# Projection and squares of chunks 0 and 1 in the idle P times V bank, at later steps, with scale and shift on GpSimd

## The reference

```
def _adaln(x, c, ...):
    sc = silu(c); shift = sc @ shift_w.T + shift_b
    scale = clip(sc @ scale_w.T + scale_b + 1.0, 0.1, 10.0)
    norm = maximum(norm_of(x, axis=-1) * 128 ** -0.5, EPS)
    return x / norm * norm_w * scale + shift
x = x + _attention(_adaln(x, c), mask, qkv_w, proj_w, proj_b)     # softmax over masked scores
x = x + silu(h1) * h2 @ w2.T + b2     # h1, h2: halves of _adaln(x, c) @ w1.T + b1
```

## Time and profile before

| what | us |
|---|---|
| three runs | 180.77, 177.42, 177.99 (median 177.99) |
| the profiled execution, its own time | 176.59 |
| its span, first to last instruction | 174.8 |
| PE / DVE / ACT / POOL busy | 148.7 / 137.9 / 134.3 / 86.7 |
| mean granted TensorE clock | 0.999 of full speed |

### The profile page before, as it was taken

How to read it: one execution, slowest core, us unless ns; L and a number is a source line. 1 busy time by engine, 2 the same in 40 slices (tenths; PEclk the granted TensorE clock), 3 DMA queues, 4 the chain that set the end, 5 groups by cost and what they waited for, 6 DMA issues and landing times.

```text
span 174.8 us, 3689 instructions
## 1 busy us (share of the span) xinstructions
PE 148.7 (85%) x1312; PEld 76.1 (44%) x1312; DVE 137.9 (79%) x234; ACT 134.3 (77%) x251; POOL 86.7 (50%) x137
## 2 busy tenths in 40 slices
PE   7979676569969999898898988897999966998992
PEld 7765233423324343333333333332236844785870
DVE  8748896978969999886998896994415938978992
ACT  8279962276869899976999977999776898698640
POOL 8319967966852134645528841246000715635650
PEclk9999999999999999999999999999999999999999
DMA  4936551517401374421021030030211200010103
GB/s 104 261 158 202 163 152 51 167 49 211 120 2 64 92 216 118 133 75 49 2 95 33 12 106 9 24 104 5 81 41 54 70 0 2 0 60 0 60 4 120
DMA packets 15336, 14.28 MB, mean 82 GB/s; under 512 B 2718, under 2 KB 14422, under 8 KB 15318
## 3 DMA queue, kind: packets, MB, share of 16 engines
q1 hardware_dynamic: 13910, 13.12, 24.9%
q0 software_dynamic: 1408, 0.93, 2.0%
HBM read 4.34 MB, written 3.15 MB: 43 GB/s over the span
## 4 chain that ended last, share of the span: by engine, by line
PE 44%; DVE 15%; ACT 15%; issue 14%; POOL 10%; DVEq 0%; ACTq 0%; POOLq 0%
ACT p_exp L1000 11%; PE bank L713 11%; PE bank L626 8%; DVE neg_max L1151 6%; POOL gated_lo L529 5%; PE bank L692 5%; PE bank L561 2%; PE bank L666 2%; PE bank L657 2%; PE bank L598 2%; POOL q_stack L493 2%; PE bank L584 2%; PE bank L763 2%; DVE rest L1126 1%; DVE k_stack L1061 1%
## 5 line engine op out<-in xcount | busy, mean ns | idle before, releaser
L1151 DVE TENSOR_REDUCE neg_max<-bank 128x2 f32<-128x512 f32 x128 | 81.6, 686 | 8.7 <-PE bank L626 7.8
L1000 ACT ACTIVATE p_exp<-bank 128x512 f32<-128x512 f32 x128 | 69.2, 594 | 9.7 <-PE bank L692 8.6
L713 PE MATMUL bank<-p_exp,v_all 128*25 128x256 f32 x512 | 40.3, 388 | 0.6
L626 PE MATMUL bank<-k_stack,q_stack 62*128 62x256 bf16 x256 | 25.2, 272 | 9.3 <-DVE neg_max L1151 7.3
L529 POOL TENSOR_TENSOR gated_lo<-rs,gated_hi 128x512 fp32r<-128x512 f32 x14 | 18.3, 1304 | 28.4 <-ACT gated_hi L1025 27.3
L493 POOL DMA_DIRECT2D q_stack<-max_rows x32 | 17.8, 558 | 26.0 <-ACT max_rows L949 22.7
L692 PE MATMUL bank<-q_stack,k_stack 64*128 64x256 bf16 x256 | 25.1, 271 | 3.8 <-ACT p_exp L1000 3.8
L626 PEld LDWEIGHTS bank<-k_stack,q_stack 62*128 62x128 bf16 x256 | 8.4, 93 | 34.3 <-DVE neg_max L1151 28.6
L692 PEld LDWEIGHTS bank<-q_stack,k_stack 64*128 64x128 bf16 x256 | 10.9, 94 | 12.3 <-ACT p_exp L1000 7.5
L713 PEld LDWEIGHTS bank<-p_exp,v_all 128*25 128x25 f32 x512 | 9.4, 102 | 15.7 <-ACT p_exp L1000 8.0
L763 PE MATMUL bank<-h_hi,w_parts 128*128 128x512 f32 x32 | 13.0, 407 | 1.6 <-DVE rs L1275 1.4
(11 more groups left out here) (117 smaller groups left out, 220.6 us busy)
## 6 DMA issues: line engine op xcount, KB each, us to landing
q_stack<-parts SPq DMA_DIRECT2D x18, 128.0 KB
k_stack<-parts SPq DMA_DIRECT2D x18, 128.0 KB
o_rows<-o_sb SPq DMA_DIRECT2D x8, 256.0 KB, 2.1
o_num<-o_rows SPq DMA_DIRECT2D x8, 128.0 KB, 2.4
o_den<-o_rows SPq DMA_DIRECT2D x8, 128.0 KB, 3.3
out_t<-o_num SPq DMA_DIRECT2D x8, 128.0 KB, 1.9
back<-back_w SPq DMA_DIRECT2D x1, 832.0 KB, 7.9
x_sb<-x_t SPq DMA_DIRECT2D x3, 256.0 KB, 5.8
```

The source lines that it names most:

```text
L626: mm = nc.tensor.matmul(scores[r][:, t * N:(t + 1) * N], q_stack[rows, c % STACKS, g, at + t * 128:at + (t + 1) * 128], k_stack[rows, c % ...
L713: mm = nc.tensor.matmul(bank[32 * j:32 * j + V_WINDOW, 6 + b % 2, half * N:(half + 1) * N], v_all[:, b, t, :, :].rearrange("p h w -> p (h ...
L1000: nc.scalar.activation(p_exp[:, u % 4, par, :, :], bank[:, RING + v % RING, :].rearrange("p (t q) -> p t q", t=KT), ACT.Exp, scale=D ** -0 ...
L1151: nc.vector.tensor_reduce(out=neg_max[:, k % 2, :, par, g], in_=bank[:, n % RING, :].rearrange("p (t k) -> p t k", t=KT), axis=AX.X, op=AL ...
```

## The change

For chunks 0 and 1:

- `project` is no item of the ring any more: it goes to the idle P times V bank (bank 6) at step 38 and 54 instead of 35 and 51, with semaphores `s_projected` and `s_y` of its own. The residual moves with it.
- `square_2` moves on POOL from k = 8 and 12 to 9 and 13; `mean_square_2` from step 38 and 54 to 46 and 62, in bank 7.
- `ln_norm_2` moves from u = 30 and 46 to 39 and 55, `inverse_norm_2` to 40 and 56, `norm_whole` from step 41 and 57 to 50 and 66. The turn that waits for `ln_norm_2` is now k = 11 and 15.
- `shifted_whole` leaves ACT and becomes two POOL `tensor_scalar` instructions (multiply by the gain column, add the shift column) ahead of `parts_h2`, which moves from k = 10 to 12 for chunk 0, and behind the whole loop of turns for chunk 1.

```diff
 P_LN_SUM, P_INVERSE_SUM, P_OVER_SUM, P_PROJECT, P_SQUARE, P_MEAN, P_LN_NORM, P_INVERSE_NORM, P_NORM, P_SHIFT, \
-    P_SECOND_PART = (7, 8, 9, 11, 12, 14, 14, 15, 17, 19, 22)
+    P_SECOND_PART = (7, 8, 9, 11, 12, 14, 23, 24, 26, 19, 22)
...
-K_OVER_SUM, K_SQUARE, K_PARTS_H2 = (3, 4, 6)
+K_OVER_SUM, K_SQUARE, K_PARTS_H2 = (3, 5, 8)
+P_PROJECT_EARLY, P_MEAN_EARLY = (14, 22)
...
 def project_position(c):
-    return BC * G * (c + 1) + LEAD + P_PROJECT
+    return BC * G * (c + 1) + LEAD + (P_PROJECT_EARLY if c < EARLY else P_PROJECT)
 def square_position(c):
-    return BC * G * (c + 1) + LEAD + P_MEAN
+    return BC * G * (c + 1) + LEAD + (P_MEAN_EARLY if c < EARLY else P_MEAN)
...
-        items += [("project", c) for c in range(NC - 1) if project_position(c) == p]
+        items += [("project", c) for c in range(EARLY, NC - 1) if project_position(c) == p]
...
+def project_bank(c):
+    return turn_bank(4 * (c + 1) + 4)
 def square_bank(c):
-    return 6 + (BC * (c + 1)) % 2
+    return turn_bank(4 * (c + 1) + 6)
...
             def square_2(c):
-                pool.wait_ge(s_ad, drained(item("project", c)))
+                pool.wait_ge(s_y, c + 1)
...
+            def shifted_whole(c):
+                if c == 0:
+                    pool.wait_ge(s_stack[NP - 1], 16 * STACK_DMAS)
+                pool.wait_ge(s_xn2, c + 1)
+                for i in range(BC):
+                    b = BC * c + i
+                    at = slice(i * N, (i + 1) * N)
+                    nc.gpsimd.tensor_scalar(h2[:, c, at], xn2[:, c, at], gain[:, b:b + 1], shift[:, b:b + 1],
+                                            ALU.mult, ALU.add).then_inc(s_h2_whole, 1)
             def parts_h2(c):
+                shifted_whole(c)
                 pool.wait_ge(s_h2_whole, BC * (c + 1))
...
+            parts_h2(EARLY - 1)
             for n in range(SPLIT_PAIRS):
...
                         if k == 4 * (c + 1) + 5:
+                            pe.wait_ge(s_y, c + 1)
+                        if k == 4 * (c + 1) + 7:
                             pe.wait_ge(s_inv2, 2 * c + 1)
...
             def project(c):
-                projected = ring_bank(item("project", c))
+                if c < EARLY:
+                    projected, done = bank[:, project_bank(c), :], s_projected
+                    pe.wait_ge(s_turned, 4 * (c + 1) + 4 - RING_TURNS + 1)
+                else:
+                    projected, done = ring_bank(item("project", c)), s_a
...
-                    pe.wait_ge(s_turned, 4 * (c + 1) + 4 - RING_TURNS + 1)
+                    pe.wait_ge(s_turned, 4 * (c + 1) + 6 - RING_TURNS + 1)
...
-            def shifted_whole(c):
-                ...
-                    nc.scalar.activation(h2[:, c, at], xn2[:, c, at], ACT.Identity,
-                                         bias=shift[:, b:b + 1], scale=gain[:, b:b + 1]).then_inc(s_h2_whole, 1)
...
-                    if p == project_position(c):
+                    if c < EARLY and p == project_position(c):
+                        dve.wait_ge(s_projected, c + 1)
+                        residual(c, project_bank(c), s_y)
+                    if c >= EARLY and p == project_position(c):
```

More of the change, by code:

```diff
@@ L280, in build @@
         s_squares = sem("s_squares")
+        s_projected = sem("s_projected")
+        s_y = sem("s_y")
         s_mp = sem("s_mp")
@@ L656, in project @@
                 pe.wait_ge(s_on, c + 1)
-                nc.tensor.matmul(projected, proj_w, o_num[:, c, :], start=True, stop=True).then_inc(s_a, 1)
+                nc.tensor.matmul(projected, proj_w, o_num[:, c, :], start=True, stop=True).then_inc(done, 1)
             def mean_square_2(c):
@@ L1017, in _ @@
                         inverse_norm_2(c)
-                    if c < NC - 2 and behind == P_SHIFT:
-                        shifted_whole(c)
             def first_part_gated(n):
```

## The result

The changed kernel takes 181.45 us in the median (180.53 to 182.27, four runs) against 178.25 for the kernel before (177.42 to 180.77, four runs). So it is about 2% slower, where 177.5 and at most 179.7 was forecast. The profiled execution took 180.98 us with a span of 179.1.

What follows compares the result with a forecast made beforehand. PE, DVE and ACT were taken as full at once in the attention loop; terms -1.2 - 1.1 - 0.6 - 0.5 + 0.2 + 1.3 + 1.1 + 0.1 = -0.7, softened to -0.5, gave 177.5 us, range 174.9 to 179.7.

Steps and rivals of the forecast that it cites:

- `norm_whole` later: At steps 50 and 66, PE's 0.54 us wait for DVE goes, twice: -1.1 us.
- an ACT stall: At step 50, chunk 0, said to cover `norm_whole`; if it isn't there, 0.5 us comes back.
- ACT's pile: Logarithm and power added onto `ln_sum` and `inverse_sum`: +1.3 us for chunk 0 before turn 12, +1.1 for chunk 1.
- The 0.61 waits for POOL: PE's waits ahead of the squares for POOL's square go, twice: -1.2 us.
- The weight split beside POOL's square: Both in POOL's turn 9, delaying the cast for the next turn: +0.2 us.
- the turns that wait for the logarithm: Turns 11 and 15 wait for a logarithm one unit old, 0.05 us each: +0.1.
- A `tensor_scalar`: Each of two POOL instructions put at 0.5 us, with room up to 0.73 at turn 12: cost 0.
- the two estimates that stood beside that: Per `tensor_scalar` of 256 columns, from the skill's page: 0.38 us at 1.8 cycles an element, 0.55 at 2.6.
- the rival on the slow side: POOL becomes the bound at turn 12, turn 13 waits if `tensor_scalar` exceeds 0.73 us: 179.8 us; chance 0.14.
- ACT absorbs the pile: Rival: logarithm and power find gaps on ACT, so +1.3 and +1.1 go: 175.1 us; chance 0.20.
- The waits move: Rival: PE's 0.61 and 0.54 waits return as other engines' idle time, half of 3.4 lost: 179.2 us; chance 0.16.
- The prediction's own sign for it: DVE waits of 0.6 us at new places would show that the waits move.

Runs made afterwards that it cites:

- norm late: The changed kernel with only `norm_whole` two units later (steps 52 and 68); median 179.23 us, beside 182.39 for the changed kernel.
- split late: The changed kernel with only the last weight split moved from POOL's turn 11 to turn 14; median 179.54 us.
- the two kernels with one part alone: The kernel before with only scale and shift on GpSimd (`K_PARTS_H2` 9), median 179.78 us; and squares at 39, 179.99 us.
- norm at 50: The changed kernel with the squares' matmul one step earlier, logarithm and power two units earlier, `norm_whole` still at step 50; median 180.03 us.
- squares at 39: The kernel before with squares' matmul, logarithm, power, norm and shift one step later; median 179.99 us, ratio 1.017.
- after again: The changed kernel run again without an edit, on the same chip as norm late; median 182.39 us.

## Why the prediction was wrong

**The step that failed** is "*`norm_whole` later* ... At the new places it is covered: step 50 lies in an ACT stall". I moved an instruction past POOL's `over_sum` and weight split and asked only what DVE, PE and ACT were doing there. Beside two POOL instructions with two SBUF inputs it isn't 0.68 long but 2.61, and the ACT stall covers only part of the 1.93 more. Its price in the changed kernel is 7.99 - 6.73 = 1.3 us from turn 11 to 12 (norm late), and most of it again by another edit (split late, 1.2). With 0.4 of DVE's time coming back at step 52, norm late is 0.9 better than the change from turn 8, and its median of ten runs, 179.23, lies inside the range that was forecast. This was mine to see: `norm_whole` has two SBUF inputs and both POOL instructions were in the trace. The Trainium skill states it, in "SBUF — State Buffer", section "Who interferes with whom": a VectorE instruction with two SBUF inputs contends with a GpSimd instruction that reads SBUF. The runs agree, by 0.68, 1.39 and 2.61 us.

**The second miss is the clock behind turn 15.** The forecast had ACT's pile there at +1.1; it measured 1.05 (11.59 against 10.54). What it didn't have is that PE's clock falls behind the waits of 0.69 and 1.26 us in four of six executions (to 0.58 over 4 us in the first), for 1.1 to 1.4 more. The 59.85 us that was forecast from turn 7 to the MLP is 2.7 short of the 62.55 measured. Of that, 1.1 lies from turn 10 to 12, with the hold (14.13, forecast 13.0), and 1.2 behind turn 15, with the fall (12.94, forecast 11.7); most of the rest, 0.3, lies ahead of turn 8, where executions vary. Without hold and fall, norm late's first profile has 54.29 from turn 8, where my schedule had 54.1 (76.1 to 130.2).

**The rest held.** The 0.61 waits for POOL went (turn 8 to 9, 6.44, forecast 6.3). The weight split beside POOL's square made no wait at turn 10: 5.22 against a plain 5.2, where I had +0.2. ACT's pile for chunk 0 was put at +1.3; undoing it gives 0.94. No wait shows at the turns that wait for the logarithm, where I had +0.1. A `tensor_scalar` takes 0.55 us, forecast 0.5; of the two estimates that stood beside that, 0.38 and 0.55, it is the second:

```profile
L467 POOL TENSOR_SCALAR parts<-o_den,gain,shift 128x256 f32<-128x256 f32 x4 | 2.2, 549 | 1.7 <-DVE o_den L1196 1.7
```

So the rival on the slow side had the right engine and the wrong mechanism: POOL never made PE wait at turn 13, it held DVE. "ACT absorbs the pile" was wrong. "The waits move" is what the two kernels with one part alone show: of 1.0 and 1.2 us in waits that went, 0.35 to 0.6 arrived, and in the second the hold took a part. The prediction's own sign for it, a wait of over 0.6 for DVE at a new place, came true as well, with the 1.44 at step 51 that the hold brought. I had counted each PE wait as worth its length.

**The size.** The medians differ by 3.2 us, and the stretch from turn 7 to the MLP by 2.4 in the first pair of profiles (2.2 to 3.0 over all of them). The first profile's other 1.8 lies in the front, ahead of the change; it is noise in the comparison and wasn't in my range for either side, which took its spread from three runs. That such noise gives the missing part of the 3.2 is argued and not shown.

## What to carry to other kernels

When an instruction moves in a hand-made order, look at what runs beside it and not only at who waits for it: find each VectorE instruction with two SBUF inputs and each GpSimd elementwise instruction near it. When three engines are full at once, put extra work where another engine's insertion has just opened a gap, and count the engine's load unit by unit: two pairs of activations on the same two units cost 0.94 us a chunk more than with one pair two units earlier. And compare from one internal mark to the next, with the same work between the marks: here most steps repeat to some hundredths of a microsecond while the whole time wanders by 5.

## What the runs showed of the hardware

- VectorE's instruction with two SBUF inputs doesn't get in between two back-to-back GpSimd instructions: started in the first, it ends 0.55 us after the second has ended (102.08 for 101.53 in the changed kernel, 101.26 for 100.71 in norm at 50), and 0.56 after a single one (101.26 for 100.70 in split late, 89.13 for 88.57 in squares at 39). GpSimd's own instructions stay at 1.28 there. Beside `norm_whole` at step 41 of the kernel before, GpSimd was issuing DMAs, and it kept its 0.68.
- It goes the other way too when VectorE is first. In norm late GpSimd's `tensor_scalar` starts 0.19 us into a VectorE `tensor_tensor` (L1270); it takes 0.92 in place of 0.55 and ends 0.42 after it. The one behind it takes 0.55 again:

```profile
130.75 0.69 DVE L1270 TENSOR_TENSOR sq<-rest 128x512 f32<-128x512 f32 x1
...
130.94 0.92 POOL L467 TENSOR_SCALAR parts<-o_den,gain,shift 128x256 f32<-128x256 f32 x1 [4.82 <-DVE o_den L1196]
...
131.86 0.55 POOL L467 TENSOR_SCALAR parts<-o_den,gain,shift 128x256 f32<-128x256 f32 x1
```

- The granted clock of TensorE fell to 0.50, the lower of its two levels, near the end of waits of 0.69 and 1.26 us (four executions of six) and behind one of 1.96 us (one of one), for 3 to 4 us. It fell between 0.3 us ahead of the end of the second wait (after again) and 1.7 us behind the end of the long one (norm at 50). The same program with the same waits kept full speed in other executions, and behind the waits of 0.94 and 1.44 us from turn 11 to 12 it fell in none of four.
